# Attention stage of a fused block kernel: VectorE's row steps spread evenly behind the groups of maskings, and the turns and the copy of the attention result put at other heads

## What is computed

```python
def _L1_xattn_ref(x, cond, mask, wq, bq, wk, bk, wv, bv, wo, bo):
    q = _w8a8_linear(x, wq, bq).reshape(B, N, H, D).transpose(0, 2, 1, 3)
    k = (cond @ wk.T + bk).reshape(B, L, H, D).transpose(0, 2, 1, 3)
    v = (cond @ wv.T + bv).reshape(B, L, H, D).transpose(0, 2, 1, 3)
    scores = jnp.einsum('bhnd,bhld->bhnl', q, k) * inv_sqrt_d + mask[:, None]
    attn = jax.nn.softmax(scores, axis=-1)
    o = jnp.einsum('bhnl,bhld->bhnd', attn, v)
    o = o.transpose(0, 2, 1, 3).reshape(B, N, C)
    return _w8a8_linear(o, wo, bo)
```

## Time and profile before

| | |
|---|---|
| Median of 3 runs | 725.24 us (724.66 to 728.22) |
| Profiled execution, its own time | 727.98 us |
| Its span, first to last instruction | 725.9 us |
| Busy in the span: TensorE, VectorE, ScalarE, GpSimd | 533.6, 365.1, 295.0, 179.8 us |
| Stage B, first scores to the meeting | 338.8 to 507.0 us |

### The profile page before, as it was taken

The page is one execution under the profiler, slowest core; times in us unless marked ns, Lnnn a source line. Parts: engine busy times, 40 slices in busy tenths (PEclk is TensorE's granted clock), DMA queues, the critical chain, the costliest instruction groups (busy, mean ns, idle before and its releaser), DMA issues. The chain is left out here.

```text
span 725.9 us, 11288 instructions
## 1 busy us (share of the span) xinstructions
PE 533.6 (74%) x3590; PEld 376.3 (52%) x3590; DVE 365.1 (50%) x962; ACT 295.0 (41%) x631; POOL 179.8 (25%) x211
## 2 busy tenths in 40 slices
PE   0060569999999999357999999994083089999991
PEld 0040557677777768233766666663073055555540
DVE  5727747755865766254677777762422022222220
ACT  4056623344344343042788888883010022222220
POOL 1001013232321322003244444423103502222221
PEclk9995569999999999758899999997555589999996
DMA  8959600000000000310122232331401515555534
GB/s 332 423 167 358 190 0 12 11 0 11 11 11 0 11 0 1 138 28 0 50 74 71 78 88 89 106 97 48 171 1 57 159 46 88 89 88 89 89 44 119
DMA packets 23075, 62.59 MB, mean 86 GB/s; under 512 B 3938, under 2 KB 9858, under 8 KB 20986
## 3 DMA queue, kind: packets, MB, share of 16 engines
q1 hardware_dynamic: 18622, 53.47, 22.1%
q0 software_dynamic: 4416, 8.63, 7.7%
HBM read 46.40 MB, written 17.32 MB: 88 GB/s over the span
## 5 line engine op out<-in xcount | busy, mean ns | idle before, releaser
L602 ACT ACTIVATE pE<-sN,nmx 100x361 f32<-100x361 f32 x128 | 77.5, 606 | 5.6 <-DVE nmx L1179 5.6
L1179 DVE CUSTOM_DVE_ANT_0 sN<-ps,maskS 100x361 f32<-100x361 f32 x128 | 62.5, 531 | 27.2 <-issue 13.4
L798 PE MATMUL ps<-ident,pE 100*121 100x100 f32 x384 | 61.8, 285 | 6.5 <-ACT pT L593 6.5
L798 PEld LDWEIGHTS ps<-ident,pE 100*121 100x121 f32 x384 | 49.5, 188 | 28.6 <-issue 18.4
L928 PE MATMUL ps<-VS,hTe 118*128 x120 | 56.7, 609 | 5.5 <-ACT hTe L640 5.5
L503 POOL DMA_INDIRECT sums_out<-yb,backI x20 | 31.1, 1554 | 108.8 <-ACT yb L650 104.8
L593 ACT COPY pT<-ps 121x300 f32<-121x300 f32 x128 | 51.4, 403 | 8.8 <-PE ps L798 8.3
L1294 DVE TENSOR_TENSOR hb<-ps,b1B 128x352 f32<-128x352 f32 x20 | 10.5, 524 | 87.8 <-PE ps L914 87.8
L914 PE MATMUL ps<-CT,xT 128*128 x160 | 52.8, 474 | 2.0 <-DVE xT L1280 2.0
L914 PEld LDWEIGHTS ps<-CT,xT 128*128 128x128 f32 x160 | 31.2, 197 | 24.9 <-issue 12.8
L1061 DVE TENSOR_REDUCE tk<-h 100x1 f32<-100x512 f32 x32 | 20.0, 679 | 40.2 <-ACT h L553 40.1
(11 more groups left out here) (237 smaller groups left out, 1177.6 us busy)
## 6 DMA issues: line engine op xcount, KB each, us to landing
VS<-in_w SPq DMA_DIRECT2D x8, 1024.0 KB, 9.3
CT<-in_ctxT SPq DMA_DIRECT2D x8, 728.0 KB, 16.6
CT<-in_ew SPq DMA_DIRECT2D x8, 704.0 KB
VS<-in_ew SPq DMA_DIRECT2D x8, 672.0 KB
slots_in<-zeros SPq DMA_DIRECT2D x5, 1056.0 KB, 12.4
xin<-slots_in SPq DMA_DIRECT2D x20, 264.0 KB, 3.4
XR<-in_x SPq DMA_DIRECT2D x1, 1600.0 KB
summB<-summary_rows SPq DMA_DIRECT2D x8, 200.0 KB
```

The source lines that it names most:

```text
L602: act.activation(pE[0:S, q, 0:T], sN[0:S, q, 0:T], ACT.Exp, scale=-1.0, bias=nmx[0:S, h_:h_ + 1], accum_out=sums[0:S, j, h_:h_ + 1]).then_ ...
L798: mm = pe.transpose(ps[0:TC, 4 + r, c * S:(c + 1) * S], pE[0:S, h_ % HPC, c * TC:(c + 1) * TC], ident[0:S, 0:S])
L1179: dve.tensor_tensor_reduce(out=sN[0:S, q, 0:T], in0=ps[0:S, q, 0:T], in1=maskS[0:S, j, 0:T], scale=-1.0, scalar=3.4e38, op0=ALU.add, op1=A ...
```

## The change

VectorE's steps are dealt out two to a place behind the maskings of heads 3, 7, 11 and 15. Statistics are taken two batches ahead, behind masking 15; the row scale of the coming batch stands behind masking 3 and its rounding behind masking 7, ahead of the normalization. The rounding of the result stands behind masking 15, and its last step behind masking 3 of the next batch. VectorE's batches are written out, where six of the eight were two bodies of a hardware loop. TensorE turns the rows and the rounded result ahead of the value products; the rounded result is turned at head 13 and multiplied at head 15 (10 and 11 before), the result is turned back at head 3 (2 before). `rows_back` waits for `y2` (VectorE's last step) in place of `x3` (GpSimd's sum). ScalarE copies the result out at head 3 and the turned result at head 14. GpSimd's body begins with the sum of b-2 and ends with the norm of b+2.

```diff
                 g.tensor_tensor(XR[0:S, b, :], y2[0:S], xbo[0:S], ALU.add).then_inc(sem("x3"), 1)
 
-            def body(b, j, u, first, last):
-                if not last:
-                    rstd_b(b + 1)
-                    norm_x(b + 1)
-                if not first:
+            def body(b):
+                if b > 1:
+                    x_out(b - 2)
+                if b:
                     with_bo(b - 1)
                     add_bv(b - 1)
-                if not last:
-                    scale_q(b + 1, 1 - j)
-                if not first:
-                    x_out(b - 1)
+                if b < B - 1:
+                    scale_q(b + 1, (b + 1) % 2)
+                if b < B - 2:
+                    rstd_b(b + 2)
+                    norm_x(b + 2)
 
             rstd_b(0)
             norm_x(0)
             scale_q(0, 0)
+            rstd_b(1)
+            norm_x(1)
             g.wait_ge(sem("bvo_in"), 48)
             for b in range(B):
-                body(b, b % 2, b // 2, b == 0, b == B - 1)
+                body(b)
+            x_out(B - 2)
             with_bo(B - 1)
             add_bv(B - 1)
             x_out(B - 1)
...
                     if h_ == 6 and not last:
                         turned_x(b + 1)
-                    if h_ == 2 and not first:
+                    if h_ == 3 and not first:
                         rows_out(b - 1)
-                    if h_ == 11 and not first:
+                    if h_ == 14 and not first:
                         turned_o(b - 1)
...
             def rows_back(b):
                 pe.wait_ge(sem("oT_out"), after(b + 1))
-                pe.wait_ge(sem("x3"), after(b))
+                if b:
+                    pe.wait_ge(sem("y2"), b)
...
                     turn_head(b, h_)
-                    if h_ % HPC == 1 and b * KC + g:
-                        mix_group(*divmod(b * KC + g - 1, KC))
-                    if h_ == 2 and b:
-                        rows_back(b - 1)
                     if h_ == 5 and b < B - 1:
                         pe.wait_ge(sem("xq2b"), b + 2)
                         pe.wait_ge(sem("o_norm"), after(b))
                         turn_rows(xq2b, "xq2_t", b + 1)
+                    if h_ == 13 and b:
+                        pe.wait_ge(sem("oQb"), after(b))
+                        if b < B - 1:
+                            pe.wait_ge(sem("q_taken"), b + 2)
+                        turn_rows(oQb, "oq_t", b - 1)
+                    if h_ % HPC == 1 and b * KC + g:
+                        mix_group(*divmod(b * KC + g - 1, KC))
+                    if h_ == 3 and b:
+                        rows_back(b - 1)
                     if h_ in (5, 9, 13):
                         for i in range(HOLD):
                             pe.matmul(ps[:, 6, KC * S:512], ident[:, :], ident[:, 0:512 - KC * S], start=True, stop=True)
                     if h_ == 7 and b < B - 1:
                         queries(b + 1)
-                    if h_ == 10 and b:
-                        pe.wait_ge(sem("oQb"), after(b))
-                        if b < B - 1:
-                            pe.wait_ge(sem("q_taken"), b + 2)
-                        turn_rows(oQb, "oq_t", b - 1)
-                    if h_ == 11 and b:
+                    if h_ == 15 and b:
                         out_rows(b - 1)
...
-            def body(b, j, u, first, last):
-                dve.wait_ge(sem(f"mask_in{j}"), 16 * u + 16)
+            def body(b):
+                j = b % 2
+                dve.wait_ge(sem(f"mask_in{j}"), 16 * (b // 2) + 16)
                 for h_ in range(HEADS):
                     q, n = h_ % HPC, b * KC + h_ // HPC
                     alone(dve, (f"score{q}", after(n + 1)), (f"exp{q}", after(n)))
@@ -1179,29 +1184,26 @@
                     dve.tensor_tensor_reduce(out=sN[0:S, q, 0:T], in0=ps[0:S, q, 0:T], in1=maskS[0:S, j, 0:T],
                                              scale=-1.0, scalar=3.4e38, op0=ALU.add, op1=ALU.min,
                                              accum_out=nmx[0:S, h_:h_ + 1]).then_inc(sem(f"masked{q}"), 1)
-                    if not first and h_ in finish_at:
-                        finish_at[h_](b - 1, 1 - j)
-                    if not last and h_ in prep_at:
-                        prep_at[h_](b + 1, 1 - j)
+                    if h_ in steps:
+                        one, of, other, on = steps[h_]
+                        if 0 <= b + of < B:
+                            one(b + of)
+                        if 0 <= b + on < B:
+                            other(b + on)
 
                 dve.tensor_copy(cols[:, 24:25], cols[:, 0:1]).then_inc(sem("mask_used"), 1)
 
 
-            def prep_rows(b, j):
-                prep_scale(b, j)
-                prep_round(b, j)
-
-            def finish_rows(b, j):
-                finish3(b, j)
-                finish4(b, j)
-
-            finish_at = {7: finish1, 11: finish_rows, 15: finish5}
-            prep_at = {3: prep_stats, 7: prep_rows, 11: prep_rescale}
-            for step in prep_at.values():
-                step(0, 0)
-            batches(dve, body)
-            for step in finish_at.values():
-                step(B - 1, (B - 1) % 2)
+            steps = {3: (prep_scale, 1, finish5, -2), 7: (prep_round, 1, finish1, -1),
+                     11: (prep_rescale, 1, finish3, -1), 15: (finish4, -1, prep_stats, 2)}
+            for step in (prep_stats, prep_scale, prep_round, prep_rescale):
+                step(0)
+            prep_stats(1)
+            for b in range(B):
+                body(b)
+            finish5(B - 2)
+            for step in (finish1, finish3, finish4, finish5):
+                step(B - 1)
             dve.wait_ge(sem("x3"), after(B))
             dve.tensor_copy(cols[:, 22:23], cols[:, 1:2]).then_inc(sem("b_done"), 1)
 
```

More of the change, by code:

```diff
@@ L1128, in row_scale, with prep_stats @@
                 ch(dve.reciprocal(inv_, scale))
-            def prep_stats(b, j):
+            def prep_stats(b):
                 chp.turn(b)
@@ L1133, in prep_stats, with prep_scale, prep_round, prep_rescale @@
                 dve.bn_aggr(mvb[0:S], st6b[0:S]).then_inc(sem("mvB"), 1)
-            def prep_scale(b, j):
+            def prep_scale(b):
                 dve.wait_ge(sem("normed"), b + 1)
                 row_scale(chp, g2[0:S], tb[0:S, 3:4], tb[0:S, 4:5], tb[0:S, 5:6])
-            def prep_round(b, j):
+            def prep_round(b):
                 chp(dve.tensor_scalar(g2[0:S], g2[0:S], tb[0:S, 5:6], MAGIC, ALU.mult, ALU.add))
                 dve.tensor_scalar(xq2b[0:S], g2[0:S], MAGIC, None, ALU.subtract).then_inc(sem("xq2b"), 1)
-            def prep_rescale(b, j):
+            def prep_rescale(b):
                 dve.wait_ge(sem("q_mm"), b + 1)
@@ L1147, in prep_rescale, with finish1 @@
                                   sxB[:].unsqueeze(1).to_broadcast([P, KC, S]), ALU.mult).then_inc(sem("q_taken"), 1)
-            def finish1(b, j):
+            def finish1(b):
                 chf.turn(b)
                 dve.wait_ge(sem("o_back"), after(b + 1))
-                chf(dve.reciprocal(rinv[0:S], sums[0:S, j]))
+                chf(dve.reciprocal(rinv[0:S], sums[0:S, b % 2]))
                 dve.tensor_tensor(oN[0:S].rearrange("p (h w) -> p h w", h=HEADS),
@@ L1156, in finish1, with finish3, finish4, finish5 @@
                                   rinv[0:S].unsqueeze(2).to_broadcast([S, HEADS, HD]), ALU.mult).then_inc(sem("o_norm"), 1)
-            def finish3(b, j):
+            def finish3(b):
                 dve.wait_ge(sem("o_biased"), b + 1)
                 row_scale(chf, oN[0:S], tb[0:S, 6:7], tb[0:S, 7:8], tb[0:S, 8:9])
-            def finish4(b, j):
+            def finish4(b):
                 chf(dve.tensor_scalar(oN[0:S], oN[0:S], tb[0:S, 8:9], MAGIC, ALU.mult, ALU.add))
                 dve.tensor_scalar(oQb[0:S], oN[0:S], MAGIC, None, ALU.subtract).then_inc(sem("oQb"), 1)
-            def finish5(b, j):
+            def finish5(b):
                 dve.wait_ge(sem("wo_mm"), b + 1)
```

## The result

| | before | after |
|---|---|---|
| Median of 6 runs each, side by side on one chip | 726.76 us | 719.45 us (718.8 to 722.44) |
| Ratio, 95% interval | | 0.9906 (0.9887 to 0.9924) |
| Median on a second chip (after: 6 runs, before: 17) | 723.84 us | 717.58 us, ratio 0.9905 (0.9889 to 0.9921) |
| Profiled execution, its own time and span | 727.98, 725.9 us | 719.32, 717.4 us |

The ratio is estimated from all runs, so it is not exactly the quotient of the two medians. The change makes the kernel faster by 0.94%. Forecast were 715 us and 1.4%; 719.45 lies inside the range, but the forecast ratio (0.986) lies outside the measured interval. The sign and the place of the gain are right, its size is about two thirds of what was forecast: 7.3 us by the medians, 6.8 by the ratio, for 10.5.

The account below looks back on a forecast made before the run. TensorE was nearest its limit, but a closed circle of hand-offs was to set the batch at 18.0 us for 19.5: six batches -9.0, batch 7 -2.0, the end +0.5, total -10.5 from 725.24, said as 715 us; range 710 to 722.

Parts of the forecast that it names:

- the waits that were named: TensorE's losses per batch: 0.33 and 0.45 around 422.07, 0.43 before 426.35, 0.64 before 428.26, 0.38 before 433.77; together 2.23 us.
- G0: Heads 0 to 3 of an attention batch, cut at the starts of the scores: forecast 4.11 us for 4.45.
- G1: Heads 4 to 7 of a batch: rows rounded before the result is normalized, rows turned at 5.87; 4.94 us for 6.03.
- the check for right: Sign that the prediction holds: ScalarE's wait before copying the turned rows is under 0.5 us, 1.19 before.
- The slower rival: VectorE's row scale behind masking 3 waits for a slower GpSimd normalization, delaying maskings 4 to 7; about 727.5 to 730, chance 0.08.
- Hand-offs eat half: Rival: some eight hand-offs in a batch each 0.1 us longer, batch 18.8 us, whole 719.5; chance 0.17.
- G2: Heads 8 to 11 of a batch, losing the result's turning and output product: forecast 4.03 us for 5.24.
- G3: Heads 12 to 15 of a batch, taking over the result's turning and output product: forecast 4.91 us for 3.78.
- Batch 7 and the end: Last attention batch, without next rows, gains 2.0 us; GpSimd's later additions cost 0.5 us at the stage's end.
- VectorE wrote them last: Before the change, next batch's rows were turned 0.36 us late because VectorE wrote them last, after the 0.95 us normalization.
- The circle: Closed chain of hand-offs from masking 15 through GpSimd, row scale, turned rows and queries back to masking 15: 18.0 us a batch.
- TensorE's own work: TensorE's work without waits, 17.3 us a batch; as a rival bound it gave 710.5 us, chance 0.13.

Follow-up runs that it names:

- before_rows_first: Kernel before, with VectorE's row scale and rounding of the next rows put ahead of the normalization of the result; 724.07 us for 723.84, ratio 1.0003.
- bias_behind_all: Changed kernel, with GpSimd's bias row computed behind the value bias instead of ahead of it; 713.52 us, 0.9845 of the kernel before.
- before_turns_only: Kernel before, with only rows turned ahead of the value products and the result copied out and turned back at head 3; 733.24 us, ratio 1.0132.
- steps_only: Changed kernel, with rows turned behind the value products and the result copied out and turned back at head 2 again; 720.89 us, 0.9954 of before.
- bias_late: Changed kernel, with GpSimd's bias row put behind the queries' two products; 713.88 us, 0.9856 of the kernel before.
- bias_one_input: Changed kernel, with GpSimd's bias row replaced by x times the constant 1, leaving out the output's bias; 715.48 us, 0.9882 of the kernel before.
- bias_stats: `bias_behind_all` plus VectorE's statistics taken ahead of the rounding of the result; 711.83 us, 0.9826 of the kernel before.
- no_filler: Changed kernel with bias row behind value bias, statistics first, result's row scale ahead of rescaling, and no filler products; 705.59 us, 0.9734 of before.

## Why the prediction was right, and where it was short

**The bound and the place of the gain: right.** The gain is in the attention batches, at the waits that were named, and the stage's layout holds: with the collision taken away, a batch is 18.09 for 18.0 and the kernel 714.0 for 714.7.

**G0: right.** 4.14 for 4.11, with the scores of head 4 waiting for a masking as laid out.

**G1: the step that failed.** "VectorE rounds the rows first (0.62 + 0.4, done 4.9), then normalizes (5.8)": the rounding took 1.27, the pair was done at 5.64 and the normalization at 6.53, and the rows were turned at 6.67 for 5.87. ScalarE waited 1.10 for the turn, where under 0.5 was the check for right. That is 0.79 us too much in each of five batches, 4.0 of the 4.2 us that the six batches fell short. The error has two halves. First, GpSimd's order was laid beside VectorE's for its own deadlines only (is the bias row done in time?), never for what runs at the same moment. The changed body calls `x_out`, `with_bo` and `add_bv` in a row, and the first waits for VectorE's last step behind masking 3; so the sum ends with the maskings 4 to 7 and the bias row starts with the rounding. Second, the row that I took as a price was not a price of the instruction alone. The summary of the kernel before has it:

```profile
L1140 DVE TENSOR_SCALAR g<-g,tb x8: 486/620/624, 331.6 to 464.2; 100x512 f32<-100x512 f32 x8
```

and GpSimd's row there, with the rounding of the earlier trace rows from 425.21 to 425.83:

```profile
424.28 1.27 POOL L442 TENSOR_TENSOR oN<-oN,bvB 100x512 f32<-100x512 f32 x1 [0.29 <-DVE oN L1154]
```

Median 620 and minimum 486 for one form: something beside it costs 0.13, and GpSimd's instruction ends at 425.55, 0.28 before. The same collision, a small piece of it, stood in the trace before.

**The slower rival** had the right pair of engines and the wrong end of it: it asked whether GpSimd's normalization gets longer beside VectorE, and answered with maskings. GpSimd's 2.10 did stay 2.10. What got longer was VectorE's rounding beside GpSimd, and the maskings said nothing of it, since they are not stretched.

**"Hand-offs eat half"** came out nearly exactly in the whole (719.5 for 719.45) and in the batch (18.8 for 18.86), but not in its reason: it spread the loss over some eight hand-offs of 0.1 us each, and the runs show one stretched instruction; with that gone, no group is over 0.2 us off. That the number fell so near this rival, and inside the range, is luck.

**G2 and G3:** 4.23 for 4.03 and 4.77 for 4.91. The maskings of heads 12 to 15 begin 0.2 later than laid out, since VectorE stands still 0.21 behind the row scale, so TensorE's wait at the scores of head 12 is 0.42 where 0.29 follows from the layout; G3's steps took 0.14 less. Together it is 0.06. **Batch 7 and the end:** 1.1 gained for 1.5. Up to its last value products batch 7 gained 1.5 for 2.0: G2 was 4.16 for 3.74, since head 12's turn waited for a copy of ScalarE (0.27), and 0.4 where 0.2 was laid out was lost behind it. The end cost 0.43 for the 0.5 forecast.

**"VectorE wrote them last"** as the reason for the late turn in the kernel before was wrong (`before_rows_first`). What fits the rows is that the row scale (1.1) left the block: without the collision the block is done 1.6 us behind the scores at head 4 (397.35 and 395.75 in `bias_behind_all`); before it was 2.8 (426.30 and 423.50). No run takes the row scale alone out of the block.

**The circle: right,** both as the length of the batch and as the reason not to forecast TensorE's own work. The Trainium skill (Perfetto Trace Analysis, Identifying the Most-Contended Engine and Optimization Strategy) would have led to 710. The changed kernel measured 719.45; once the collision was gone and two links of the circle were shortened, TensorE's work was the bound, and 0.9791 x 725.24 = 710.1 us. That rule gave the end point of this order of work, and the circle said how much of the way one change goes.

**A slower case was left out:** the turns ahead of the value products with rows that come late, behind which the clock can fall (`before_turns_only`, +1.3%). In the changed kernel the wait is 0.86 where that kernel had 1.43, and the granted clock stayed full in its batches 1 to 6; how near it is to a fall was not tried.

Attribution of a batch, each number a measured batch: 19.50 before, 18.97 with VectorE's and GpSimd's order and the place of the output product, 18.86 with the turns, 18.09 without the collision, 17.82 with the statistics first, 17.22 with the row scale inside the wait, 16.80 without fillers. The single steps hold only in this order: the turns are worth 0.11 here because the collision hides what they bring, and most of the 0.77 that its end gives back needs the turns (G1 of `steps_only` is 5.60 with the collision and without).

**Open.** `steps_only` is 0.49% slower than the changed kernel, 3.5 us. Its profile shows 2.7 of it: 1.33 in batch 1, 0.5 in the five behind it, 0.1 in batch 0 and 0.7 in batch 7 with the end; the rest is within the intervals of the two ratios. Batch 0 has a few microseconds of half clock in some profiled executions and not in others: it took 18.65 before, 18.54 and 20.07 in two executions of the changed kernel, and 15.72 or 15.73 in five kernels whose profile shows no fall, `bias_behind_all` among them. What decides that was not tried; for this reason the kernels are compared by medians, and by their profiles only in batches at full clock.

## What to carry to other kernels

When steps are moved on two engines that run side by side, lay the engines' timelines over each other and look at what runs at the same moment, not only at who waits for whom; here the pair VectorE rounding and GpSimd addition cost over a third of the gain, and one line moved on GpSimd gave it back. Before a duration is taken as a price, read the minimum and the median of all instructions of that form: where they differ, another engine is already in it. A turn or product is better put ahead of covering work only if its input is ready: here it brought nothing otherwise, and the clock fell behind the uncovered wait in half of the batches. And what a part of a change is worth can't be read from one order of undoing: the turns seemed worth 0.1 us a batch as long as another delay stood in the same group.

## What the runs showed of the hardware

A fp32 `tensor_scalar` of 100 x 512 on VectorE, from SBUF to SBUF, takes 0.48 us alone. Beside a GpSimd `tensor_tensor` (both inputs in SBUF) that began before it, it ends 0.28 to 0.29 us behind that instruction's end, wherever it starts, if its own 0.48 would not take it further: 419.44 behind 419.15 (changed kernel), 425.83 behind 425.55 (before), 422.34 behind 422.06 (`bias_late`), 401.04 behind 400.76 (`steps_only`). Maskings (one input in PSUM) and reductions kept their 0.53 and 0.67 to 0.69 also where GpSimd had begun before them: reductions of 0.69 at 358.67 beside the bias row from 358.60 (changed kernel), and of 0.68 at 422.60 beside the one from 422.09 (`before_rows_first`).

The Trainium skill (SBUF — State Buffer, Who interferes with whom) says that VectorE and GpSimd share a pair of SBUF ports as an exclusive lock, that `tensor_scalar` can take both pairs and then contends, that `tensor_reduce` on trn2 never does, and that the loser "fully blocks" for the whole instruction. The trace agrees on the pairing and on the end of the blocking, 0.28 us behind GpSimd's. The first step of `bias_one_input`, 0.61 us beside a GpSimd instruction of 1.50, doesn't fit "fully blocks". The other side of the pair is in `bias_stats`: GpSimd's small addition (L382) takes 0.72 there, beside VectorE's second rounding step, which began before it, and 0.57 otherwise.

The granted clock fell from 2.4 to 1.2 GHz behind a single wait of 1.43 or 1.44 us of a TensorE that was busy before, in three of the six batches of `before_turns_only`; behind the same wait in the other three it stayed at 2.4. Behind the waits of 0.86 in the changed kernel and of 0.42 in `no_filler` it fell in none of batches 1 to 6.
